# A graph-attention kernel on one core: the cross scores of two tiles packed into one 128x128 square and turned by one product instead of two

## The chip, the cores and the metric

The kernel runs on one core of a Trainium2 chip. A core has four computing engines that matter here: TensorE (PE in the profile; its weight loads have a row of their own, PEld), VectorE (DVE), ScalarE (ACT) and GpSimd (POOL). SyncE (SP) starts the transfers. Each engine works through its own list of instructions in order and waits on semaphores that others raise. The metric is the device time of the whole program in microseconds (us), lower is better; the median of three runs is given.

## What is computed

There are 128 graphs of 64 nodes, each node a row of 384 numbers, and one 64x64 adjacency matrix for each graph. A layer norm with a relu comes first, then two graph layers in a row, an addition to the input, another layer norm with a relu, a third graph layer, and a last addition. Each of the three graph layers does this:

```python
u = h @ h.T / sqrt(384)                      # 64 x 64 scores of a graph
a = softmax(u); delta = a * adjacency
attn = delta / (sum(delta) + 1e-10)
ctx = (attn above the diagonal) @ (h @ Wl.T + bl) \
    + diag(attn) * (h @ Ws.T + bs) \
    + (attn below the diagonal) @ (h @ Wr.T + br)
o = relu((ctx - mean) / sqrt(var + eps) * g + beta)
```

The three graph layers are the kernel's three phases. In all of them the scores are symmetric apart from rounding, which is split below.

## The kernel before

A tile is 128 rows, that is two graphs; a step handles two tiles (k = 0, 1), and a phase has 32 steps, so the program has 96. Each `body(s)` is one step, and on every engine the order of the calls in `body` is the order in which the engine works. Most steps of a phase run from a hardware loop of two bodies, the first two and the last four are written out. Work of several steps is interleaved: while step s is projected, step s+1 (`nxt`) is scored and masked, the output of step s-1 (`prev`) is normed, and the inputs of steps s+2 to s+4 are prepared.

Numbers are carried as a rounded part HI and a remainder LO, so every projection takes three products for each of three chunks of 384. One step on PE, in order: right projection of tile 0, `weigh` (attention times the projected rows) of the last step's tile 1, left and self projection of tile 0, the scores of `nxt` (six products of 256 columns), right projection of tile 1, `turn_cross(nxt)`, `weigh` of tile 0, left and self projection of tile 1. In phase 1 the left projection of tile 1 also has `spread_max` in it, a single product of 128 columns. `weigh` waits for `side_hi` and `side_lo` of the right side, does three products, waits for those of the left side and does three more. `side_lo` is what DVE's `split_side` raises (L828).

The scores of a tile pair need the term HI times HI plus HI times LO plus its mirror image. `scores` multiplies HI of a tile with HI and LO side by side, so `score_bank` holds for each tile a 128x128 square of HI.HI and a 128x128 square of HI.LO, the cross scores. The mirror image of the cross scores is made in four moves: ACT copies both squares to `cross` (`copy_cross`, L568, 128x256), PE turns them by a product with the identity and adds them onto the HI.HI squares in `score_bank` (`turn_cross`, L430, two products of 128 columns), and DVE adds the two (`sum_scores`, L764, one instruction for each half of the partitions) into `score`. Only the two 64x64 blocks on the diagonal of each square are scores of a graph; the others are left unused.

After that `score` goes on: in phases 0 and 2 (`bounded`) ACT takes the exponential straight away (`exponentials`, L585), and DVE masks it (`mask_edges`, L793). In phase 1 the row maximum comes first (`row_maximum` L771, `place_max` L776, `spread_max` on PE, `shift_scores` L785). POOL builds the edge blocks from the masked scores (L1010, L1014).

Other lines that are named below: on DVE L743 `turn_nodes` (waits for ACT's `fill_source`, L552 or L549), L726 `input_stats` (phases 0 and 2), L852 `centre`, L861 `norm`, L870 `residual` (phases 1 and 2), L730 the first instruction of `gather_input`, L747 `split_nodes`; on ACT L609 `split_side` and L603 `seed_side`; on PE L447 the projections and L478 `weigh`.

Of the kernel before, what the change touches and what calls it, by code (L numbers as in the profile page):

```python
# [32 lines left out]
F32 = mybir.dt.float32  # L33
# [5 lines left out]
P = 128  # L39
NODES = 64  # L40
# [87 lines left out]
def adj_gnn_program(nc, x, adj, weights, vectors, identity, triangles, out):  # L128
# [6 lines left out]
    with ctx:  # L135
# [55 lines left out]
        edge_bank = bank("edge_bank")  # L191
        first_bank = [edge_bank, score_bank]
        max_rows = edge_bank[:, 0:2 * NODES].rearrange("p (k i) -> p k i", k=2)
        score_copy = cross[:, :, 0:NODES]
        scores4 = score_bank[:, :].rearrange("p (k a j) -> p k a j", k=2, a=2)
        source = nodes[:, :].rearrange("p (k d) -> p k d", k=2)
# [36 lines left out]
        node_hi = sem("node_hi")  # L233
        node_lo = sem("node_lo")
        scored = sem("scored")
        cross_copied = sem("cross_copied")
        cross_turned = sem("cross_turned")
        score_summed = sem("score_summed")
        max_done = sem("max_done")
        max_placed = sem("max_placed")  # L240
# [164 lines left out]
        def _(pe):  # L405
            def transpose_first(s):
                at_least(pe, score_summed, 2 * s.n)
                for k in range(2):
                    pe.wait_ge(source_ready, s.tile(k) + 1)
                    for c in range(CH):  # L410
                        mm = nc.tensor.transpose(first_bank[k][:, c * P:(c + 1) * P], source[:, k, c * P:(c + 1) * P], ident)
                    mm.then_inc(first_moved, 1)
# [12 lines left out]

            def turn_cross(s):

                pe.wait_ge(cross_copied, s.n + 1)
                for k in range(2):
                    mm = nc.tensor.matmul(score_bank[:, k * 256:k * 256 + P], cross[:, k], ident_r[:, :],  # L430
                                          start=False, stop=True, skip_group_check=True)
                mm.then_inc(cross_turned, 1)

            def spread_max(s):

# [103 lines left out]
        def _(act):  # L539
# [24 lines left out]

            def copy_cross(s):
                act.wait_ge(scored, s.n + 1)
                at_least(act, score_summed, 2 * s.n)
                nc.scalar.activation(cross[:, :, :], scores4[:, :, 1, :], ACT.Copy).then_inc(cross_copied, 1)  # L568

            def totals(s):  # L570
                act.wait_ge(max_bias_done, s.n + 1 - PAIRS)
# [5 lines left out]
            def exponentials(s):  # L577
                if not s.bounded:
                    act.wait_ge(shift_done, s.n + 1 - PAIRS)
                    nc.scalar.activation(score[:, :, :], score[:, :, :], ACT.Exp, scale=SCALE).then_inc(exp_done, 2)  # L580
                    return
                act.wait_ge(score_summed, 2 * s.n + 2)
                at_least(act, den_done, s.tile(0) - 2)
                for k in range(2):
                    nc.scalar.activation(score[:, k], score[:, k], ACT.Exp, scale=SCALE,  # L585
                                         accum_out=total[:, s.parity, k:k + 1]).then_inc(exp_done, 1)
# [132 lines left out]
        def _(dve):  # L719
# [39 lines left out]

            def sum_scores(s):  # L760

                dve.wait_ge(cross_turned, s.n + 1)
                for h, half in enumerate(HALVES):
                    nc.vector.tensor_tensor(score[half], scores4[half, :, 0, h * NODES:(h + 1) * NODES],  # L764
                                            cross[half, :, h * NODES:(h + 1) * NODES].bitcast(F32),
                                            ALU.add).then_inc(score_summed, 1)

            def row_maximum(s):

                dve.wait_ge(score_summed, 2 * s.n + 2)  # L770
                nc.vector.tensor_reduce(row_max[:, :], score[:, :, :], op=ALU.max, axis=AX.X).then_inc(max_done, 1)  # L771

            def place_max(s):
# [104 lines left out]
            def first_step(s):  # L878
                nxt, second, third, fourth = s.ahead(1), s.ahead(2), s.ahead(3), s.ahead(4)
                split_side(s, 0, RIGHT)  # L880
                sum_scores(s)
                split_side(s, 0, LEFT)
                mask_edges(s)
                gather_stats(second)
                split_first(SELF)
                split_first_nodes(nxt)
                input_shift(second)
                diagonal(s)
                split_edges(s)
                gather_stats(third)  # L890
                turn_nodes(second)
                input_shift(third)
                split_side(s, 1, RIGHT)
                split_side(s, 1, LEFT)
                sum_scores(nxt)
                context_stats(s, 0)
                denominator(s, 0)
                turn_nodes(third)
                gather_moments(s, 0)
                mask_edges(nxt)  # L900
                centre(s, 0)
                gather_stats(fourth)
                input_shift(fourth)

            def body(s):
# [17 lines left out]
                split_edges(s)  # L923
                if prev.exists():
                    centre(prev, 1)
                if fourth.exists() and fourth.bounded:
                    input_stats(fourth, 0)
                    input_stats(fourth, 1)
                if prev.exists():
                    norm(prev, 0)  # L930
                if nxt.exists():
                    sum_scores(nxt)
                if nxt.exists() and not nxt.bounded:
                    row_maximum(nxt)
                    place_max(nxt)
# [153 lines left out]
```

## Time and profile before

| | |
|---|---|
| median of 3 runs | 1234.78 us (1233.87 to 1236.38) |
| the profiled execution, its own time | 1234.55 us |
| its span in the trace | 1232.8 us |
| PE busy | 1215.1 us, 99% |
| PE weight loads busy | 1208.2 us |
| DVE busy | 1089.1 us, 88% |
| ACT busy | 833.8 us, 68% |
| POOL busy | 323.5 us, 26% |
| granted PE clock, mean | 0.997 |

The time outside the span, 1.75 us, is the start and the end of the program. Busy shares are means over the whole span; the phases differ in what they ask of DVE, and the phases can be told apart by time: phase 0 runs to about 412 us, phase 1 to about 820 us, phase 2 to the end.

### The profile page before, as it was taken

What the parts mean: (1) busy time and instruction counts of PE and PEld (TensorE: products, weight loads), DVE (VectorE), ACT (ScalarE), POOL (GpSimd) and SP (SyncE); (2) the same over time, 40 slices, a digit from 0 to 9 for tenths busy, and PEclk for the clock granted to TensorE, in tenths of its full rate; (3) what the DMA queues carried; (4) which work ended last, traced back from release to release, by engine and by line L of the source; (5) the groups of instructions that cost most, each with busy time, mean ns of one, the idle gap of its engine ahead of it and who ended that gap; (6) DMA issues with size and microseconds to landing.
All of it is one profiled execution on the core that took longest, in us unless ns stands there. A gap on an engine that the chain in (4) does not pass through costs nothing.

```text
span 1232.8 us, 27495 instructions
## 1 busy us (share of the span) xinstructions
PE 1215.1 (99%) x7163; PEld 1208.2 (98%) x7163; DVE 1089.1 (88%) x3125; ACT 833.8 (68%) x2079; POOL 323.5 (26%) x438
## 2 busy tenths in 40 slices
PE   8999999999999999999999999999999999999997
PEld 7899999999999999999999999999999999999997
DVE  7888888888887889999999999999999999999986
ACT  6666666666767776666667676676666666666763
POOL 2322222222222221212112121342323232323221
PEclk9999999999999999999999999999999999999999
DMA  5433333333233333232323333432332323232331
GB/s 187 127 109 94 107 96 101 101 92 110 88 106 122 102 109 107 96 106 84 105 94 99 103 96 106 144 98 95 96 106 96 106 96 106 96 101 95 97 96 43
DMA packets 112899, 126.91 MB, mean 103 GB/s; under 512 B 11104, under 2 KB 100192, under 8 KB 112864
## 3 DMA queue, kind: packets, MB, share of 16 engines
q1 hardware_dynamic: 112864, 126.50, 32.9%
q8 instruction: 15, 0.25, 0.1%
q14 instruction: 20, 0.16, 0.0%
HBM read 76.91 MB, written 49.55 MB: 103 GB/s over the span
## 4 chain that ended last, share of the span: by engine, by line
PE 91%; DVE 3%; issue 3%; POOL 1%; DMA 1%; ACT 0%; SPq 0%; POOLq 0%; DVEq 0%; ACTq 0%
PE left_bank L447 23%; PE right_bank L447 23%; PE context_bank L447 23%; PE context_bank L478 16%; PE score_bank L422 5%; PE score_bank L430 1%; DMA rows<-weights 1%; DVE node_t L747 1%; DVE context L861 0%; POOL weight L1021 0%; DVE turned L743 0%; DVE in_stats L726 0%; DVE context L852 0%; DVE side_parts L828 0%; DVE score L764 0%
## 5 line engine op out<-in xcount | busy, mean ns | idle before, releaser
L447 PE MATMUL left_bank<-weight,node_t 128*128 128x384 f32 x1728 | 337.9, 338 | 0.0
L447 PE MATMUL context_bank<-weight,node_t 128*128 128x384 f32 x1728 | 332.7, 337 | 3.2 <-ACT context_bank L615 3.2
L447 PE MATMUL right_bank<-weight,node_t 128*128 128x384 f32 x1728 | 333.7, 338 | 1.0 <-ACT right_bank L603 0.6
L609 ACT ACTIVATE side_parts<-right_bank 128x384 fp32r<-128x384 f32 x192 | 94.4, 492 | 316.6 <-PE context_bank L478 316.6
L447 PEld LDWEIGHTS context_bank<-weight,node_t 128*128 128x128 f32 x1728 | 303.5, 189 | 3.7 <-ACT context_bank L615 3.5
L447 PEld LDWEIGHTS left_bank<-weight,node_t 128*128 128x128 f32 x1728 | 303.9, 188 | 0.0
L447 PEld LDWEIGHTS right_bank<-weight,node_t 128*128 128x128 f32 x1728 | 298.9, 188 | 2.1 <-issue 1.8
L478 PE MATMUL context_bank<-side_parts,attn_t 128*128 128x386 f32 x1152 | 240.7, 344 | 3.7 <-issue 3.4
L478 PEld LDWEIGHTS context_bank<-side_parts,attn_t 128*128 128x128 f32 x1152 | 199.0, 190 | 6.6 <-issue 5.7
L747 DVE TENSOR_TENSOR node_t<-nodes,node_t 128x768 fp32r<-128x768 f32 x94 | 119.8, 1275 | 18.1 <-ACT node_t L557 18.1
L1004 POOL TENSOR_TENSOR rstd<-spread,scalars 128x2 f32<-128x2 f32 x96 | 66.2, 689 | 257.6 <-DVE spread L844 257.6
L1014 POOL TENSOR_TENSOR edge_block<-edge,tri 128x512 f32<-128x512 f32 x96 | 133.3, 1388 | 0.0
L743 DVE STREAM_TRANSPOSE turned<-nodes 128x768 f32<-128x768 f32 x94 | 91.9, 978 | 44.4 <-ACT nodes L552 41.3
L621 ACT ACTIVATE context_bank<-context_bank,diag 128x386 f32<-128x386 f32 x192 | 105.1, 547 | 34.4 <-PE context_bank L447 33.6
L1010 POOL TENSOR_TENSOR own_edge<-edge,tri 128x128 f32<-128x128 f32 x96 | 46.8, 488 | 306.1 <-DVE edge L793 306.1
L852 DVE SCALAR_TENSOR_TENSOR context<-context_bank,moments,vector_rows 128x384 f32<-128x384 f32 x192 | 117.0, 609 | 2.4
L833 DVE BATCH_NORM_STATS2 stats<-context_bank 128x6 f32<-128x384 f32 x192 | 107.1, 558 | 12.0 <-PE context_bank L478 11.9
L828 DVE TENSOR_TENSOR side_parts<-right_bank,side_parts 128x384 fp32r<-128x384 f32 x192 | 106.6, 555 | 12.2 <-ACT side_parts L609 8.4
L828 DVE TENSOR_TENSOR side_parts<-left_bank,side_parts 128x384 fp32r<-128x384 f32 x192 | 102.7, 535 | 2.1 <-ACT side_parts L609 2.1
L998 POOL TENSOR_TENSOR in_spread<-in_moments,scalars 128x2 f32<-128x2 f32 x64 | 17.7, 277 | 304.4 <-DVE in_moments L731 304.4
L615 ACT ACTIVATE context_bank<-vector_rows 128x386 f32<-128x386 f32 x192 | 94.5, 492 | 0.0
L603 ACT ACTIVATE left_bank<-vector_rows 128x384 f32<-128x384 f32 x192 | 93.6, 488 | 0.0
(75 smaller groups left out, 1520.5 us busy)
## 6 DMA issues: line engine op xcount, KB each, us to landing
squares<-turned SPq DMA_DIRECT2D x94, 384.0 KB, 2.7
nodes<-squares SPq DMA_DIRECT2D x376, 96.0 KB, 2.2
rows<-x SPq DMA_DIRECT2D x64, 384.0 KB, 3.7
out<-rows SPq DMA_DIRECT2D x31, 384.0 KB, 2.6
adj_in<-adj SPq DMA_DIRECT2D x96, 64.0 KB, 1.9
piece<-weights SPq DMA_DIRECT2D x18, 192.0 KB, 2.6
rows<-weights SPq DMA_DIRECT2D x3, 576.0 KB, 7.8
vector_rows<-vectors SPq DMA_DIRECT2D x3, 384.0 KB, 7.0
```

The costliest lines, as they stand in the source:

```text
L447: mm = nc.tensor.matmul(bank[:, 0:D], node_t[:, s.parity, k, c, a], weight[:, s.phase % 2, w, c, b], start=False, stop=(c, a) == (CH - 1, ...
L478: mm = nc.tensor.matmul(context_bank[k][:, 0:DX], attn_t[:, a, k, 1 - side], side_parts[:, side, b], start=False, stop=(side == LEFT and a ...
L603: nc.scalar.activation(side_bank[side][k][:, 0:D], vector_row(s.phase, ROW_LEFT + side), ACT.Copy)\
L609: nc.scalar.activation(side_parts[:, side, HI, 0:D], side_bank[side][k][:, 0:D], ACT.Copy).then_inc(side_hi[side], 1)
L615: nc.scalar.activation(context_bank[k][:, 0:DX], vector_row(s.phase, ROW_SELF, 2), ACT.Copy)\
L621: nc.scalar.activation(context_bank[k][:, 0:DX], context_bank[k][:, 0:DX], ACT.Identity, scale=diag[:, s.parity, k:k + 1]).then_inc(self_s ...
L743: nc.vector.transpose(turned[:, :, :], source_blocks).then_inc(nodes_turned, 1)
L747: nc.vector.tensor_tensor(node_rows(s, LO), moved_rows, node_rows(s, HI).bitcast(F32), ALU.subtract).then_inc(node_lo, 1)
L828: nc.vector.tensor_tensor(side_parts[:, side, LO, 0:D], side_bank[side][k][:, 0:D], side_parts[:, side, HI, 0:D].bitcast(F32), ALU.subtrac ...
L833: nc.vector.bn_stats(stats[:, k], context_bank[k][:, 0:D]).then_inc(stats_done, 1)
L852: nc.vector.scalar_tensor_tensor(context[:, k], context_bank[k][:, 0:D], moments[:, k, 0:1], vector_row(s.phase, ROW_GAMMA), ALU.subtract, ...
L1014: nc.gpsimd.tensor_tensor(edge_block[:, :, :, :].rearrange("p k u (h j) -> p k (u h) j", h=2), edge[:, :, :].unsqueeze(2).to_broadcast([P, ...
```

## The change

`copy_cross` no longer copies both 128x128 cross squares. It copies only the diagonal blocks: two instructions (64 partitions, 2x64 elements) take, for each half of the partitions, the block that stands in its own half for both tiles, and two more (64 partitions, 64 elements) put those blocks of the first and last place where a packed square needs them. `cross[:, ...]` is looked at as four blocks of 64 columns, and the middle two are `cross_pack`, one 128x128 square with the four cross blocks of both tiles. `turn_cross` turns that square by one product, into the last 128 columns of `edge_bank`, with nothing added to it. `sum_scores` adds HI.HI and the copied cross block from `cross`, in two instructions as before, but it now waits for the four copies and no longer for PE. A new `add_cross` adds the turned block, one DVE instruction of 128x128 that reads `score` and `edge_bank`.

In DVE's `body`, `sum_scores(nxt)` moves ahead of `input_stats(fourth)` and `norm(prev, 0)`, and `add_cross(nxt)` stands where `sum_scores(nxt)` stood.

```diff
+        cross_blocks = cross[:, :, :].rearrange("p a (b j) -> p (a b) j", b=2)
+        cross_pack = cross_blocks[:, 1:3].rearrange("p b j -> p (b j)")
+        cross_here = [cross_blocks[half, 1 - h:4 - h:2] for h, half in enumerate(HALVES)]
+        turned_cross = edge_bank[:, 3 * P:4 * P].rearrange("p (k j) -> p k j", k=2)
...
             def turn_cross(s):
-                pe.wait_ge(cross_copied, s.n + 1)
-                for k in range(2):
-                    mm = nc.tensor.matmul(score_bank[:, k * 256:k * 256 + P], cross[:, k], ident_r[:, :],
-                                          start=False, stop=True, skip_group_check=True)
-                mm.then_inc(cross_turned, 1)
+                pe.wait_ge(cross_packed, 4 * (s.n + 1))
+                at_least(pe, cross_added, s.n)
+                nc.tensor.matmul(edge_bank[:, 3 * P:4 * P], cross_pack, ident_r[:, :],
+                                 start=True, stop=True, skip_group_check=True).then_inc(cross_turned, 1)
...
             def copy_cross(s):
                 act.wait_ge(scored, s.n + 1)
+                at_least(act, cross_turned, s.n)
                 at_least(act, score_summed, 2 * s.n)
-                nc.scalar.activation(cross[:, :, :], scores4[:, :, 1, :], ACT.Copy).then_inc(cross_copied, 1)
+                for h, half in enumerate(HALVES):
+                    nc.scalar.activation(cross_here[h], scores4[half, :, 1, half], ACT.Copy).then_inc(cross_packed, 1)
+                for h, half in enumerate(HALVES):
+                    nc.scalar.activation(cross_blocks[HALVES[1 - h], 1 + h], scores4[half, 1 - h, 1, half], ACT.Copy).then_inc(cross_packed, 1)
...
             def sum_scores(s):
-                dve.wait_ge(cross_turned, s.n + 1)
-                for h, half in enumerate(HALVES):
-                    nc.vector.tensor_tensor(score[half], scores4[half, :, 0, h * NODES:(h + 1) * NODES],
-                                            cross[half, :, h * NODES:(h + 1) * NODES].bitcast(F32),
-                                            ALU.add).then_inc(score_summed, 1)
+                dve.wait_ge(cross_packed, 4 * (s.n + 1))
+                for h, half in enumerate(HALVES):
+                    nc.vector.tensor_tensor(score[half], scores4[half, :, 0, half], cross_here[h].bitcast(F32),
+                                            ALU.add).then_inc(score_summed, 1)
+
+            def add_cross(s):
                 dve.wait_ge(cross_turned, s.n + 1)
+                dve.wait_ge(score_summed, 2 * s.n + 2)
+                nc.vector.tensor_tensor(score[:, :, :], score[:, :, :], turned_cross, ALU.add).then_inc(cross_added, 1)
```

The places that waited for `score_summed` before the exponentials and the row maximum now wait for `cross_added`; `transpose_first`, used at the program's start, waits for it too.

Instructions on DVE in the loop of phase 2, from L743 of one step on. Before:

```order
L743 STREAM_TRANSPOSE turned<-nodes 128x768
L828 TENSOR_TENSOR side_parts<-left_bank,side_parts 128x384
L821 TENSOR_TENSOR attn_t<-edge_block,attn_t 128x512
L852 SCALAR_TENSOR_TENSOR context<-context_bank,moments,vector_rows 128x384
L726 BN_STATS in_stats<-rows 128x6 x2
L861 SCALAR_TENSOR_TENSOR context<-context,rstd,vector_rows 128x384
L764 TENSOR_TENSOR score<-score_bank,cross 64x128 x2
L730 MEMSET scalars 128x1
```

And now, where the numbers of the lines have moved (L773 is `sum_scores`, L735 `input_stats`, L780 `add_cross`):

```order
L752 STREAM_TRANSPOSE turned<-nodes 128x768
L842 TENSOR_TENSOR side_parts<-left_bank,side_parts 128x384
L835 TENSOR_TENSOR attn_t<-edge_block,attn_t 128x512
L866 SCALAR_TENSOR_TENSOR context<-context_bank,moments,vector_rows 128x384
L773 TENSOR_TENSOR score<-score_bank,cross 64x128 x2
L735 BN_STATS in_stats<-rows 128x6 x2
L875 SCALAR_TENSOR_TENSOR context<-context,rstd,vector_rows 128x384
L780 TENSOR_TENSOR score<-score,edge_bank 128x128
L739 MEMSET scalars 128x1
```

The two sums stand three instructions earlier, and one instruction of 128x128 is new in their old place; nothing behind it has changed places.

Instructions on ACT in the loop of phase 0, from the scaling of tile 1's self rows to the next wait for PE. Before:

```order
L621 ACTIVATE context_bank<-context_bank,diag 128x386
L566 REGISTER_ALU
L98 REGISTER_ALU
L568 ACTIVATE cross<-score_bank 128x256
L603 ACTIVATE left_bank<-vector_rows 128x384
```

And now:

```order
L630 ACTIVATE context_bank<-context_bank,diag 128x386
L571 REGISTER_ALU
L98 REGISTER_ALU
L575 ACTIVATE cross<-score_bank 64x2x64 x2
L577 ACTIVATE cross<-score_bank 64x64 x2
L612 ACTIVATE left_bank<-vector_rows 128x384
```

One copy has become four shorter ones; the seed behind them, and the wait behind that, stand where they stood.

## Rows read from the trace of the kernel before

**Rows 1.** Windows, phases 0 to 2: length; busy PE, PEld, DVE, ACT, POOL; clock; DMA.

```profile
200.00:300.00 100.00, 100.00 (x596) 100.00 (x595) 83.98 (x258) 68.21 (x169) 26.44 (x40) 1.00 0.34 100
500.00:600.00 100.00, 100.00 (x598) 100.00 (x597) 94.55 (x249) 68.39 (x175) 18.81 (x24) 1.00 0.32 100
1000.00:1100.00 100.00, 100.00 (x594) 99.70 (x593) 91.44 (x274) 67.97 (x168) 30.14 (x41) 1.00 0.31 100
```

**Rows 2.** Timeline of phase 0, PE: start us, us, what; the start counts.

```profile
313.89 0.33 PE L430 MATMUL score_bank<-ident_r,cross 128*128 128x128 f32 x2
...
315.18 1.74 PE L447 MATMUL left_bank<-weight,node_t 128*128 128x384 f32 x9
319.88 1.21 PE L478 MATMUL context_bank<-side_parts,attn_t 128*128 128x386 f32 x6
320.93 1.74 PE L447 MATMUL left_bank<-weight,node_t 128*128 128x384 f32 x9
```

**Rows 3.** Timeline of phase 1, PE, around the single product of 128 columns.

```profile
617.70 0.22 PE L437 MATMUL edge_bank<-max_diag,same_graph 128*128 128x128 f32 x1
...
618.34 1.74 PE L447 MATMUL context_bank<-weight,node_t 128*128 128x384 f32 x9
```

**Rows 4.** Timeline of phase 2, ACT's copies and exponentials, PE's load for `turn_cross`.

```profile
1006.84 0.39 ACT L568 ACTIVATE cross<-score_bank 128x256 fp32r<-128x256 f32 x1
1007.12 0.49 ACT L603 ACTIVATE left_bank<-vector_rows 128x384 f32<-128x384 f32 x1
1007.97 0.37 PEld L430 LDWEIGHTS score_bank<-ident_r,cross 128*128 128x128 f32 x2
1010.50 0.25 ACT L585 ACTIVATE score<-score 128x64 f32<-128x64 f32 x1
```

**Rows 5.** Timeline of phase 1, DVE, `sum_scores` of two steps and neighbours.

```profile
602.29 0.60 DVE L861 SCALAR_TENSOR_TENSOR context<-context,rstd,vector_rows 128x384 f32<-128x384 f32 x1
603.14 0.61 DVE L764 TENSOR_TENSOR score<-score_bank,cross 64x128 f32<-64x128 f32 x2 [0.24 <-PE score_bank L430]
...
615.01 0.61 DVE L861 SCALAR_TENSOR_TENSOR context<-context,rstd,vector_rows 128x384 f32<-128x384 f32 x1
615.73 0.61 DVE L764 TENSOR_TENSOR score<-score_bank,cross 64x128 f32<-64x128 f32 x2
616.37 0.28 DVE L771 TENSOR_REDUCE row_max<-score 128x2 fp32r<-128x128 f32 x1
```

**Rows 6.** Timeline of phase 2, DVE and PEld, in order of time.

```profile
1005.21 0.98 DVE L743 STREAM_TRANSPOSE turned<-nodes 128x768 f32<-128x768 f32 x1 [0.77 <-ACT nodes L552]
...
1007.15 0.61 DVE L852 SCALAR_TENSOR_TENSOR context<-context_bank,moments,vector_rows 128x384 f32<-128x384 f32 x1
...
1009.78 0.06 DVE L730 MEMSET scalars<- 128x1 f32 x1
...
1013.92 0.55 DVE L828 TENSOR_TENSOR side_parts<-left_bank,side_parts 128x384 fp32r<-128x384 f32 x1
...
1014.31 0.74 PEld L478 LDWEIGHTS context_bank<-side_parts,attn_t 128*128 128x128 f32 x4
1014.58 0.47 PEld L478 LDWEIGHTS context_bank<-side_parts,attn_t 128*128 128x128 f32 x3
...
1017.71 0.98 DVE L743 STREAM_TRANSPOSE turned<-nodes 128x768 f32<-128x768 f32 x1 [0.75 <-ACT nodes L552]
```

**Rows 7.** Timeline of DVE near phase 1's end, `norm` and `sum_scores`.

```profile
792.67 0.60 DVE L861 SCALAR_TENSOR_TENSOR context<-context,rstd,vector_rows 128x384 f32<-128x384 f32 x1
793.19 0.60 DVE L764 TENSOR_TENSOR score<-score_bank,cross 64x128 f32<-64x128 f32 x2
...
807.19 0.60 DVE L764 TENSOR_TENSOR score<-score_bank,cross 64x128 f32<-64x128 f32 x2
```

**Rows 8.** Timeline of DVE, phase 1, `shift_scores`, of the new instruction's shape.

```profile
619.33 0.29 DVE L785 TENSOR_TENSOR score<-score,edge_bank 128x128 f32<-128x128 f32 x1
619.64 0.56 DVE L870 SCALAR_TENSOR_TENSOR rows<-context,rows 128x384 f32 x1
```

More of the change, by code:

```diff
@@ L235, in adj_gnn_program @@
         scored = sem("scored")
-        cross_copied = sem("cross_copied")
+        cross_packed = sem("cross_packed")
         cross_turned = sem("cross_turned")
+        cross_added = sem("cross_added")
         score_summed = sem("score_summed")
@@ L426, in turn_cross @@
             def turn_cross(s):
-                pe.wait_ge(cross_copied, s.n + 1)
-                for k in range(2):
-                    mm = nc.tensor.matmul(score_bank[:, k * 256:k * 256 + P], cross[:, k], ident_r[:, :],
-                                          start=False, stop=True, skip_group_check=True)
-                mm.then_inc(cross_turned, 1)
+                pe.wait_ge(cross_packed, 4 * (s.n + 1))
+                at_least(pe, cross_added, s.n)
+                nc.tensor.matmul(edge_bank[:, 3 * P:4 * P], cross_pack, ident_r[:, :],
+                                 start=True, stop=True, skip_group_check=True).then_inc(cross_turned, 1)
             def spread_max(s):
@@ L581, in exponentials @@
                     return
-                act.wait_ge(score_summed, 2 * s.n + 2)
+                act.wait_ge(cross_added, s.n + 1)
                 at_least(act, den_done, s.tile(0) - 2)
@@ L760, in sum_scores @@
             def sum_scores(s):
+                dve.wait_ge(cross_packed, 4 * (s.n + 1))
[3 more added lines that the diff above has]
+            def add_cross(s):
                 dve.wait_ge(cross_turned, s.n + 1)
-                for h, half in enumerate(HALVES):
-                    nc.vector.tensor_tensor(score[half], scores4[half, :, 0, h * NODES:(h + 1) * NODES],
-                                            cross[half, :, h * NODES:(h + 1) * NODES].bitcast(F32),
-                                            ALU.add).then_inc(score_summed, 1)
+                dve.wait_ge(score_summed, 2 * s.n + 2)
+                nc.vector.tensor_tensor(score[:, :, :], score[:, :, :], turned_cross, ALU.add).then_inc(cross_added, 1)
             def row_maximum(s):
-                dve.wait_ge(score_summed, 2 * s.n + 2)
+                dve.wait_ge(cross_added, s.n + 1)
                 nc.vector.tensor_reduce(row_max[:, :], score[:, :, :], op=ALU.max, axis=AX.X).then_inc(max_done, 1)
@@ L881, in first_step @@
                 sum_scores(s)
+                add_cross(s)
                 split_side(s, 0, LEFT)
@@ L895, in first_step @@
                 sum_scores(nxt)
+                add_cross(nxt)
                 context_stats(s, 0)
@@ L925, in body @@
                     centre(prev, 1)
+                if nxt.exists():
+                    sum_scores(nxt)
                 if fourth.exists() and fourth.bounded:
@@ L931, in body @@
                 if nxt.exists():
-                    sum_scores(nxt)
+                    add_cross(nxt)
                 if nxt.exists() and not nxt.bounded:
```

## The prediction

> **What bounds the kernel now.** I read the windows first, one from the middle of each phase [rows 1]. PE is busy for the whole 100 us in all three, at the full granted clock; the weight loads are too, except in phase 2, where 0.3 us are missing. DVE is at 84, 95 and 91 of 100. So PE sets the pace, but DVE is a close second in phases 1 and 2, and what the change takes from PE it gives to DVE. The question for each phase is whether DVE, or a chain through DVE, has a shorter period than PE will have.
>
> I read that from the timeline. In phase 1 the only place where DVE waits for PE is `sum_scores`: `norm` starts at 615.01 and `sum_scores` 0.72 us later, in the other step at 602.29 and 0.85 us later [rows 5]. Where DVE does not wait, the two stand 0.52 us apart (792.67 to 793.19, [rows 7]; rows of 0.6 us overlap by some 0.08). So DVE idles 0.20 and 0.33 us, 0.27 on average, in a step of 12.59 (603.14 to 615.73, [rows 5]). Everything else that DVE waits for in that phase is POOL or ACT work that DVE itself released. **DVE's own period in phase 1 is about 12.59 - 0.27 = 12.32 us.**
>
> In phase 2 DVE has a visible wait at L743 of 0.77 and 0.75 us, for ACT's `nodes` [rows 6]. It looks like slack and is not. From L743 at 1005.21 DVE runs without a stop to `split_side` of the left side, which ends at 1013.92 + 0.55 = 1014.47. PE, in the middle of `weigh`, starts its third load at 1014.31 and the fourth, the one that needs this result, at 1014.58: 0.27 us later where 0.175 is normal. So PE already waits about 0.1 us for DVE here. When `weigh` is done ACT can read the next right projection and seed, and the `nodes` that it writes after that release L743 at 1017.71. That is a **closed chain**, L743 on DVE, left split, `weigh` on PE, ACT, L743, and its period is 1017.71 - 1005.21 = 12.50 us. In the next step PE does not wait, by a hair, so PE and the chain tie. Phase 0 has no `residual` on DVE and no such tie: DVE has 16 us in 100, some 2 us a step, free [rows 1].
>
> **The change part by part.**
>
> *PE loses one product of 128 columns a step.* The two now cost 315.18 - 313.89 = 1.29 us with the `weigh` behind them, and a `weigh` without them takes 320.93 - 319.88 = 1.05 [rows 2], so 0.24 for two. What one alone costs in this stream is shown by `spread_max`: from 617.70 to 618.34 are 0.64 us for it and three projections at 1.05 / 6 = 0.175, which leaves 0.115 [rows 3, 2]. Saved: 0.24 - 0.12 = **0.12 us a step**.
>
> The Trainium skill's page "TensorE: Matmul & The Clock Gate", section "Back-to-back issue gap", gives about 81 ns for each load and product of 128 columns in a sustained stream; by that the saving would be 0.08 us a step and the total some 1.2 us later than mine. The row of this kernel is dearer, and I go by the row.
>
> *ACT makes four copies instead of one.* A copy of 128x256 takes 0.39 us and the next starts after 0.28, so rows overlap by 0.11; one of 64 elements takes 0.25 [rows 4]. Between them, 128 elements take about 0.30. Two starts at 0.20 apart, one at 0.15, and a last row of 0.25 put the end at 0.20 + 0.20 + 0.15 + 0.25 = 0.80 us behind the start. PE's load for `turn_cross` stands 1007.97 - 1006.84 = 1.13 us behind it [rows 4], so PE does not wait, with 0.33 to spare. ACT's extra 0.45 us lie ahead of its long wait for PE and cost nothing.
>
> *DVE gets `add_cross` and moves the sums.* Its shape stands in phase 1 already: `shift_scores`, 128x128 out of `score` and `edge_bank`, takes 0.29 us and holds the next one up for 0.31 [rows 8]. Bounds: 0.19 us if it overlaps as other rows do (0.1 less), 0.32 if the next one depends on it, as `row_maximum` does. The sums read what they read before and keep 0.61 us for two. In phase 2 they now come up at 1007.15 + 0.52 = 1007.67, when the four copies end at 1006.84 + 0.80 = 1007.64 and their semaphore has still to arrive: 0 to 0.1 us of waiting. Before, L852 to L730 takes 1009.78 - 1007.15 = 2.63 us [rows 6] for `centre`, two `input_stats`, `norm` and two sums; the same ones stand there after, in another order, and the add's 0.31 come on top. So **DVE pays 0.31 us a step**, with 0.2 to 0.4 for the bounds and the wait together. It no longer waits for PE at this place.
>
> **The sum, by stages**, against the profiled 1234.55 us.
> - Phase 0, 31 steps: DVE's 0.31 lie in its 2 us, PE saves 0.12: **-3.7**.
> - Phase 1, 28 steps up to where input statistics start again: PE would need 12.59 - 0.12 = 12.47, DVE 12.32 + 0.31 = 12.63. DVE is late by 0.16 a step until the gap to PE is used up, two steps, and from then on sets the pace: 26 x (12.63 - 12.59) = +1.0, -0.2 for the first two: **+0.8**.
> - Four steps around the start of phase 2, which are DVE-bound now (807.19 - 793.19 = 14.00 us for a step, the sums 0.52 behind `norm`, so no wait for PE, [rows 7]): 4 x 0.31 = **+1.2**.
> - Phase 2, 26 steps: the chain goes through `add_cross` but not through `turn_cross`, which PE does elsewhere in the step, while ACT and DVE work. It pays the 0.31 and gets nothing back, less some 0.02 because in every other step it does not bind yet: 12.50 + 0.29 = 12.79, and 26 x 0.29 = **+7.5**.
> - The last four steps have no inputs to prepare, DVE has room: **-0.5**.
>
> Together +5.3: 1234.55 + 5.3 = 1239.9, **1240 us**. The profiled run is 0.2 us below the median, so that holds for the median too. 0.2% of this kernel, 2.5 us, is about what a measurement can tell from no change.
>
> **The rivals.**
> - *DVE's cost is small* (the add overlaps, 0.15 to 0.2 us in all). Phase 1 then stays with PE: 12.32 + 0.18 = 12.50 against 12.59, -2.5; phase 2 gets 0.18 - 0.02 = 0.16 longer, x 26 = +4.2; with -3.7, +0.7 and -0.5 that is -1.8, 1233 us. For it: in most rows of DVE the next starts early. Against it: the same shape, `shift_scores`, does not [rows 8].
> - *DVE's waits are real slack, PE is the only bound* (the other side: faster). Then all steps but the four save 0.12: 92 x 0.12 = 11, 1223.5 us. For it: PE is at 100 of 100 and DVE waits 0.75 us a step in phase 2. Against it: the late fourth load [rows 6]. It decides from the point where the chain of phase 2 has 0.3 us of room.
> - *The copies are late.* If each holds ACT up as long as the 128x256 one does, 0.28, the last ends at 3 x 0.28 + 0.30 = 1.14 us, a hundredth behind PE's load, and with the semaphore PE waits 0.1 a step and gives back what it saved; the sums in phase 2 wait another 0.35. That gives 0 + 0.8 + 1.2 + 26 x 0.64 = +18.6, 1253 us. Against it: ACT's rows shorten with their length [rows 4].
> - *The new waits tie POOL's work to DVE's in a worse way.* `mask_edges` and POOL's edge blocks come 0.3 us later in phase 0; were 0.3 a step exposed there, 31 x 0.3 = +9, 1249 us. The free 2 us speak against it.
>
> **How the numbers follow.** My forecast (chain of phase 2 pays, 1236 to 1244) 0.60; small DVE cost, 1230 to 1236, 0.17; PE alone, 1224, 0.07; late copies, 0.08; POOL, 0.04; something not seen, either way, 0.04. Leaving out PE alone and half of the dearest gives 1230 to 1249. Faster by over 0.2% (below 1232.3): 0.07 + a third of 0.17 + 0.02 = 0.14. Within 0.2%: the rest of the small cost and the lowest of my own, 0.17. Slower: 0.69.
>
> **What the profile after would show.** In phase 0 a step of 12.35 us with PE still at 100 of 100. In phase 1 no wait of DVE at the sums or the add, and PE waiting in `weigh` for the left split, step 12.6 to 12.65. In phase 2 PE's gap before the fourth load of `weigh` growing from 0.1 to about 0.4 us, a step near 12.8, while L743 keeps its wait of 0.75. The four copies ending 0.8 us behind the first one's start, ahead of PE's load. I am wrong if phase 2's step stays under 12.6, which happens if the add takes less than 0.15 us of DVE's time or if PE reaches the fourth load with room that I misread, or if PE waits for `cross_packed`.

## The result

The changed kernel takes 1243.98 us (median of 6 runs, 1243.53 to 1245.62); the kernel before, timed beside it, 1235.51 us (6 runs, 1233.87 to 1236.83). The ratio is 1.0073, 95% interval 1.0061 to 1.0085: **slower by 8.5 us**. I had said 1240.0, between 1230 and 1249, and most likely slower (0.69).

The profiled execution took 1245.62 us, span 1243.8 us, the highest of the six, 1.6 us above the median; that of before was 1.0 us below its median. So the two traces differ by 11.0 us where the medians differ by 8.5. The stages behind the 4th product make up 8.1 of the 11.0; of the start's 2.9 the medians leave about 0.4, known only to some 1.5 either way. Stages are compared by the starts of numbered products of `turn_cross` (1st, 4th, 32nd, 61st, 65th, 91st, 96th), and most of the excess stands before the 4th.

| us between starts | before | after | difference | predicted |
|---|---|---|---|---|
| program start to the 4th | 52.09 | 55.02 | +2.9 | -0.4 |
| phase 0, 28 steps | 349.08 | 345.72 | -3.36 | -3.4 |
| phase 1, 29 steps | 365.31 | 366.32 | +1.0 | +0.8 |
| four steps around the start of phase 2 | 53.83 | 55.74 | +1.9 | +1.2 |
| phase 2, 26 steps | 325.22 | 333.10 | +7.9 | +7.5 |
| last five | 62.40 | 63.18 | +0.8 | -0.5 |

The windows of the three phases after the change, same columns as [rows 1]:

```profile
200.00:300.00 100.00, 100.00 (x594) 100.00 (x593) 86.72 (x266) 74.57 (x196) 26.71 (x41) 1.00 0.33 100
500.00:600.00 100.00, 100.00 (x586) 98.23 (x585) 95.87 (x255) 72.10 (x199) 18.55 (x23) 1.00 0.32 100
1000.00:1100.00 100.00, 98.19 (x571) 95.88 (x570) 91.29 (x276) 70.81 (x188) 29.25 (x39) 1.00 0.31 99
```

Phase 0 is still PE's alone, with both rows at 100. In phase 1 the weight loads have gaps, and DVE is at 96. In phase 2 PE itself has gaps now: the row that stood at 100 is at 98.19, and the loads went from 99.70 to 95.88. DVE's share did not rise there, though it has more to do: it waits longer too.

The timeline of phase 0, PE, `scores` of two steps in a row (start, length, what):

```profile
299.66 0.87 PE L428 MATMUL score_bank<-node_t 128*128 128x256 f32 x6
...
312.00 0.87 PE L428 MATMUL score_bank<-node_t 128*128 128x256 f32 x6
```

12.34 us a step; 28 steps of before took 349.08, or 12.467 each, and 28 of after 345.72, or 12.347. The product that went is worth 0.120 us.

The timeline of phase 2 after the change, DVE, ACT and PEld, one step (answers to [rows 4] and [rows 6]):

```profile
1011.94 0.98 DVE L752 STREAM_TRANSPOSE turned<-nodes 128x768 f32<-128x768 f32 x1 [0.77 <-ACT nodes L557]
...
1013.57 0.57 ACT L575 ACTIVATE cross<-score_bank 64x128 fp32r<-64x128 f32 x2
1013.88 0.61 DVE L866 SCALAR_TENSOR_TENSOR context<-context_bank,moments,vector_rows 128x384 f32<-128x384 f32 x1
1014.16 0.46 ACT L577 ACTIVATE cross<-score_bank 64x64 fp32r<-64x64 f32 x2
...
1014.66 0.61 DVE L773 TENSOR_TENSOR score<-score_bank,cross 64x128 f32<-64x128 f32 x2 [0.17 <-ACT cross L577]
1014.70 0.19 PEld L436 LDWEIGHTS edge_bank<-ident_r,cross 128*128 128x128 f32 x1
...
1016.23 0.60 DVE L875 SCALAR_TENSOR_TENSOR context<-context,rstd,vector_rows 128x384 f32<-128x384 f32 x1
...
1016.87 0.29 DVE L780 TENSOR_TENSOR score<-score,edge_bank 128x128 f32<-128x128 f32 x1
...
1017.72 0.55 DVE L842 TENSOR_TENSOR side_parts<-right_bank,side_parts 128x384 fp32r<-128x384 f32 x1
...
1020.57 0.54 PEld L483 LDWEIGHTS context_bank<-side_parts,attn_t 128*128 128x128 f32 x3
1021.01 0.55 DVE L842 TENSOR_TENSOR side_parts<-left_bank,side_parts 128x384 fp32r<-128x384 f32 x1
...
1021.67 0.47 PEld L483 LDWEIGHTS context_bank<-side_parts,attn_t 128*128 128x128 f32 x3 [0.55 <-issue]
...
1024.80 0.98 DVE L752 STREAM_TRANSPOSE turned<-nodes 128x768 f32<-128x768 f32 x1 [0.74 <-ACT nodes L557]
```

Three things are to be seen. L752 keeps its wait of 0.77 and 0.74 us while the step grows to 12.86 us here: the wait is part of the circle and no slack. The chain's end is where it was forecast: the left split ends at 1021.56 and the fourth load of `weigh` starts at 1021.67, and PEld stood idle for 0.55 us before it. And what was not forecast: the four copies end at about 1014.62, 1.05 us behind the first one's start, and the sums, which would have started 0.52 us behind `centre` at 1014.40, start at 1014.66. **DVE loses 0.26 us to ACT in each step**, inside the chain (the row shows 0.17 of it as idle; the rest is the overlap with `centre` that is lost). PE's load for `turn_cross` at 1014.70 just does not wait.

### The profile page after: what moved, and what is told of

Same layout as the page of the kernel before. It is cut to its first block, busy times and chain, and to the rows that moved or that the text cites. A ratio compares the mean times of both kernels' runs of the same rounds, so it can differ in the third digit from the quotient of the medians.

```text
span 1243.8 us, 28008 instructions
## 1 busy us (share of the span) xinstructions
PE 1216.8 (98%) x7067; PEld 1195.4 (96%) x7067; DVE 1111.1 (89%) x3221; ACT 893.6 (72%) x2367; POOL 323.6 (26%) x438
## 4 chain that ended last, share of the span: by engine, by line
PE 45%; issue 24%; DVE 19%; ACT 5%; POOL 3%; DVEq 2%; DMA 0%; ACTq 0%; POOLq 0%; SPq 0%
PE right_bank L452 11%; PE context_bank L452 11%; PE left_bank L452 11%; PE context_bank L483 8%; DVE context L875 4%; PE score_bank L428 3%; DVE side_parts L842 3%; DVE stats L847 2%; DVE context L866 2%; POOL edge_block L1032 1%; DVE node_t L756 1%; POOL own_edge L1028 1%; ACT nodes L557 1%; DVE in_stats L735 1%; DVE score L773 1%
## 5 line engine op out<-in xcount | busy, mean ns | idle before, releaser
L483 PE MATMUL context_bank<-side_parts,attn_t 128*128 128x386 f32 x1152 | 248.6, 347 | 10.1 <-DVE side_parts L842 6.8
L483 PEld LDWEIGHTS context_bank<-side_parts,attn_t 128*128 128x128 f32 x1152 | 195.9, 189 | 24.1 <-issue 20.9
L752 DVE STREAM_TRANSPOSE turned<-nodes 128x768 f32<-128x768 f32 x94 | 91.9, 978 | 43.7 <-ACT nodes L557 40.7
L630 ACT ACTIVATE context_bank<-context_bank,diag 128x386 f32<-128x386 f32 x192 | 104.8, 546 | 25.9 <-PE context_bank L452 25.3
L612 ACT ACTIVATE right_bank<-vector_rows 128x384 f32<-128x384 f32 x192 | 91.8, 478 | 0.8 <-DMA vector_rows<-vectors 0.8
```

The source lines that it names most:

```text
L483: mm = nc.tensor.matmul(context_bank[k][:, 0:DX], attn_t[:, a, k, 1 - side], side_parts[:, side, b], start=False, stop=(side == LEFT and a ...
L612: nc.scalar.activation(side_bank[side][k][:, 0:D], vector_row(s.phase, ROW_LEFT + side), ACT.Copy)\
L630: nc.scalar.activation(context_bank[k][:, 0:DX], context_bank[k][:, 0:DX], ACT.Identity, scale=diag[:, s.parity, k:k + 1]).then_inc(self_s ...
L752: nc.vector.transpose(turned[:, :, :], source_blocks).then_inc(nodes_turned, 1)
```

## The experiments

All were timed beside the kernel before on the same chip. Its median was 1235.66 us (25 runs) beside the first four, 1235.13 (29) beside the next four and 1235.02 (15) beside the last two. Each kernel ran 8 to 10 times, one_product 4 and mixed 5. Line numbers shift by a few between kernels. The stages of all of them, in us as in the table above:

| kernel | to the 4th | phase 0 | phase 1 | four | phase 2 | last five |
|---|---|---|---|---|---|---|
| before | 52.09 | 349.08 | 365.31 | 53.83 | 325.22 | 62.40 |
| after | 55.02 | 345.72 | 366.32 | 55.74 | 333.10 | 63.18 |
| one_product | 53.80 | 345.72 | 361.66 | 53.72 | 324.38 | 62.05 |
| dve_only | 52.12 | 349.08 | 365.47 | 54.63 | 327.71 | 62.68 |
| two_copies | 54.68 | 345.72 | 366.04 | 55.14 | 326.76 | 62.33 |
| old_place | 53.47 | 345.72 | 363.17 | 55.22 | 327.78 | 62.46 |
| act_more | 54.37 | 349.08 | 365.36 | 53.86 | 325.24 | 62.40 |
| packed0 | 54.36 | 345.72 | 365.21 | 53.85 | 325.25 | 62.41 |
| packed01 | 54.46 | 345.72 | 363.32 | 55.21 | 325.28 | 62.42 |
| add_first | 54.43 | 345.72 | 362.19 | 54.40 | 329.18 | 62.65 |
| mixed | 54.20 | 345.72 | 362.22 | 54.39 | 325.21 | 62.40 |
| two_waits | 52.61 | 349.08 | 365.31 | 53.94 | 325.18 | 62.37 |

**one_product**: PE's part of the change alone, on the kernel before (tile 1 goes without the mirror image of its cross scores).

```diff
-                for k in range(2):
+                for k in range(1):
                     mm = nc.tensor.matmul(score_bank[:, k * 256:k * 256 + P], cross[:, k], ident_r[:, :],
```

> The kernel before with one of the two turning products left out (the cross scores of tile 1 are not turned, so its scores are not the reference's); DVE and ACT do what they did. My theory: 0.12 us a step saved where PE is the bound, in phase 0 (-3.7) and phase 1 (-3.4, since DVE's 12.33 us there are below PE's 12.47), nearly nothing in phase 2 where the chain already ties (12.46 against 12.50, -1), -0.5 in the last four steps: -8 to -9 us, 1227 us. The rival, PE alone is the bound: 92 x 0.12, -11 us, 1224 us. If the product costs only what its 0.08 us from start to start say: -5 us, 1230 us.

Measured 1227.32 us, ratio 0.9927 (0.9911 to 0.9944). Phase 0 gives the full 0.120 us a step, phase 1 0.126 (365.31 - 361.66 over 29), phase 2 only 0.03 (325.22 - 324.38 over 26). PE alone would take 12.347 us a step if its work there is that of phase 0, and phase 2 takes 12.476: there the chain sets the step, and with PE relieved nothing more is to be had. With two products PE alone would take 12.467 and the step is 12.508, 0.03 us above the chain's own. "DVE's waits are real slack" falls here.

**dve_only**: the kernel before, with an addition of the new one's shape behind the sums (it adds columns of the unturned cross scores once more).

```diff
+                dve.wait_ge(score_summed, 2 * s.n + 2)
+                nc.vector.tensor_tensor(score[:, :, :], score[:, :, :], scores4[:, :, 1, 0:NODES], ALU.add).then_inc(cross_added, 1)
```

> The kernel before with one DVE instruction more, of the shape of add_cross and at its place, and nothing taken from PE or added to ACT (it adds the first 64 columns of each unturned cross square once more to the scores, so the scores are not the reference's). My theory, that DVE's own period binds in phase 1 and the chain through the left split in phase 2: PE gives nothing, phase 0 stays at 12.47 us a step, phase 1 gets about 0.1 us a step longer, phase 2 about 0.3, the four steps between them 0.3 each, in all +9 to +11 us, 1245 us. The rival, that DVE's waits are slack and PE alone is the bound: within 1 us of before.

Measured 1238.56 us, ratio 1.0026 (1.0016 to 1.0035): +2.9 us where I expected three times that. The timeline of its phase 2, DVE:

```profile
1009.41 0.61 DVE L855 SCALAR_TENSOR_TENSOR context<-context_bank,moments,vector_rows 128x384 f32<-128x384 f32 x1
...
1011.38 0.60 DVE L765 TENSOR_TENSOR score<-score_bank,cross 64x128 f32<-64x128 f32 x2
1012.01 0.29 DVE L769 TENSOR_TENSOR score<-score,score_bank 128x128 f32<-128x128 f32 x1
1012.23 0.18 DVE L732 BATCH_NORM_AGGREGATE in_moments<-in_stats 128x2 f32<-128x6 f32 x1
...
1013.02 0.55 DVE L831 TENSOR_TENSOR side_parts<-right_bank,side_parts 128x384 fp32r<-128x384 f32 x1
```

The add takes 0.29 us, but what follows starts 0.22 behind it, and of that some is won back before the right split. From `centre` to the right split are 3.61 us here and 3.47 in one_product (1013.66 to 1017.13): the add costs the chain **0.14 us** and not 0.31. The rows of one_product:

```profile
1013.66 0.60 DVE L852 SCALAR_TENSOR_TENSOR context<-context_bank,moments,vector_rows 128x384 f32<-128x384 f32 x1
...
1017.13 0.56 DVE L828 TENSOR_TENSOR side_parts<-right_bank,side_parts 128x384 fp32r<-128x384 f32 x1
```

Phase 1, where I expected 0.1 us a step, grew by 0.16 us in all 29.

**two_copies**: the kernel after, in which ACT makes both copies of the lower half first and each sum waits only for the two copies of its half.

```diff
-                dve.wait_ge(cross_packed, 4 * (s.n + 1))
                 for h, half in enumerate(HALVES):
+                    dve.wait_ge(cross_packed, 4 * s.n + 2 * h + 2)
...
                     nc.scalar.activation(cross_here[h], scores4[half, :, 1, half], ACT.Copy).then_inc(cross_packed, 1)
-                for h, half in enumerate(HALVES):
```

> The changed kernel with the four copies reordered, both that read the lower half of the partitions first, and the first sum waiting for two copies and the second for four, so DVE does not wait at the sums. If the copies' lateness (0.26 us between where the sums could start and where they do in phase 2) is part of what makes phase 2 slow: 0.2 us a step back there, 26 steps, -5 us against the changed kernel, 1239 us, phases 0 and 1 as they were. If only the add's own time counts: no change from 1244 us.

Measured 1236.7 us, ratio 1.0012 (1.0002 to 1.0021), 7.3 us below after's median, more than the 5 that I expected. The copies still end late, and DVE no longer waits for them, in the timeline of phase 2:

```profile
1008.83 0.27 ACT L575 ACTIVATE cross<-score_bank 64x128 fp32r<-64x128 f32 x1
1009.12 0.21 ACT L576 ACTIVATE cross<-score_bank 64x64 fp32r<-64x64 f32 x1
1009.36 0.27 ACT L575 ACTIVATE cross<-score_bank 64x128 fp32r<-64x128 f32 x1
1009.66 0.22 ACT L576 ACTIVATE cross<-score_bank 64x64 fp32r<-64x64 f32 x1
```

```profile
1009.14 0.61 DVE L865 SCALAR_TENSOR_TENSOR context<-context_bank,moments,vector_rows 128x384 f32<-128x384 f32 x1
1009.66 0.60 DVE L772 TENSOR_TENSOR score<-score_bank,cross 64x128 f32<-64x128 f32 x2
...
1012.72 0.55 DVE L841 TENSOR_TENSOR side_parts<-right_bank,side_parts 128x384 fp32r<-128x384 f32 x1
```

Phase 2 loses 6.3 of its 7.9 us, the four steps 0.6 of 1.9 and the last five 0.85, all they had. **The wait for the copies was most of the change's cost.**

**old_place**: the kernel after, with the two sums back behind `norm`, right ahead of the add.

```diff
-                if nxt.exists():
-                    sum_scores(nxt)
                 if fourth.exists() and fourth.bounded:
                     input_stats(fourth, 0)
...
                 if nxt.exists():
+                    sum_scores(nxt)
                     add_cross(nxt)
```

> The changed kernel with the two sums put back in their old place, right ahead of the add. DVE then doesn't wait for the copies, and the add no longer starts 0.12 us late behind the norm. My theory: phase 2 loses the 0.26 us wait and gains a little at the add, about 12.66 us a step in place of 12.85, -5 us; phase 1 hardly moves; 1239 us. The rival, that moving the sums early is what keeps the cost of the add down (its operands are ready): slower than 1244 us by 0.1 us a step, 1250 us.

Measured 1235.27 us, ratio 0.9996 (0.9986 to 1.0005): better than expected, and 8.7 us below after. There is no wait for copies in this place, and `centre` to the right split is 3.62 us (1005.80 to 1009.42), as in dve_only. Phase 1 gains too, 366.32 to 363.17: there the order was the cost, since no wait for copies shows in after. With the add in this place DVE's step in phase 1 is at most 363.17 / 29 = 12.52 us.

**act_more**: the kernel before, with two copies of 64 partitions ahead of the full copy.

```diff
+                for h, half in enumerate(HALVES):
+                    nc.scalar.activation(cross[half, :, half], scores4[half, :, 1, half], ACT.Copy).then_inc(first_copies, 1)
+                act.wait_ge(first_copies, 2 * s.n + 2)
                 nc.scalar.activation(cross[:, :, :], scores4[:, :, 1, :], ACT.Copy).then_inc(cross_copied, 1)
```

> The kernel before with two copies of 64 partitions and 2x64 elements ahead of the full copy on ACT, some 0.65 us more of ACT a step, the full copy ending about 1.05 us behind the first one's start, ahead of PE's load at 1.13; DVE and PE as before. My theory, that ACT's time there is hidden by its wait for PE: within 1 us of 1235.7. The rival, that the later start of the seed behind it or of the turn reaches PE: 0.1 us a step or more, 1245 us.

Measured 1235.2 us, ratio 0.9999 (0.9989 to 1.0008): more work on ACT, and a seed that starts later, cost nothing from the 4th product on. In phase 2 the full copy ends 0.99 us behind the first one's start (1009.21 to 1010.20), and PE's load stands at 1010.34, so the turn itself was not late. What is left for the copies of after is DVE's wait.

**packed0** and **packed01**: the kernel old_place in phase 0, or in phases 0 and 1; the code of before in the rest.

```diff
+                if s.phase >= 1:
+                    pe.wait_ge(cross_copied, s.n + 1 - 1 * PAIRS)
+                    for k in range(2):
+                        mm = nc.tensor.matmul(score_bank[:, k * 256:k * 256 + P], cross[:, k], ident_r[:, :],
+                                              start=False, stop=True, skip_group_check=True)
+                    mm.then_inc(cross_turned, 1)
+                    return
```

with the like in `copy_cross` and `sum_scores`, and no `add_cross` there.

> Packed copies, one product and the add in phase 0 only, the sums in their old place; phases 1 and 2 as in the kernel before. My theory: phase 0 gives 3.4 us from the 4th to the 32nd step, 1 to 2 us of it go in the program's first 50 us, nothing changes after: 1233.5 us. The rival, that the start takes nothing on average: 1232 us.

> Packed in phases 0 and 1, old form in phase 2, the sums in their old place. My theory: phase 0 -3.4, phase 1 -2.1 (363.2 in place of 365.3 us for 29 steps, DVE's own period there being 12.52), the start +1 to +2, phase 2 as before: 1231.5 us, faster than both kernels. The rival, that DVE's load in phase 1 spoils the steps around phase 2's start by as much: 1234 us.

Measured: packed0 1232.09 us, ratio 0.9976 (0.9965 to 0.9987), at the rival's 1232; packed01 1233.1, 0.9984 (0.9975 to 0.9994), nearer to its rival's 1234 than to my 1231.5. Packing pays where PE alone sets the pace. In phase 1 packed01 gains 2.0 us and gives 1.4 back in the four steps behind, which DVE sets; in all, nothing that shows in the medians.

**add_first**: two_copies with the add ahead of `norm` instead of behind it.

```diff
+                if nxt.exists():
+                    add_cross(nxt)
                 if prev.exists():
                     norm(prev, 0)
-                if nxt.exists():
-                    add_cross(nxt)
```

> The changed kernel with the copies in the order of two_copies and the add ahead of the norm instead of behind it, in all phases. In the runs so far the add never starts before the norm ahead of it has ended (0.65 us behind its start, where 0.52 is usual). If that 0.12 us is the price of this neighbour: phase 1 at 12.50 us a step in place of 12.62 (-3.4 us against two_copies), phase 2 by 0.0 to 0.1 us a step shorter, 1232 to 1233 us. If the price goes with the add wherever it stands: 1236.7 us, as two_copies.

Measured 1234.33 us, ratio 0.9990 (0.9980 to 1.0000), a little above what I expected. Against two_copies phase 1 fell by 3.85 us, to 0.5 us above one_product's; phase 2 rose by 2.4. The timeline of phase 2, DVE, shows why:

```profile
1005.57 0.61 DVE L865 SCALAR_TENSOR_TENSOR context<-context_bank,moments,vector_rows 128x384 f32<-128x384 f32 x1
1006.09 0.60 DVE L772 TENSOR_TENSOR score<-score_bank,cross 64x128 f32<-64x128 f32 x2
1006.72 1.02 DVE L734 BATCH_NORM_STATS2 in_stats<-rows 128x6 f32 x2
1007.77 0.29 DVE L779 TENSOR_TENSOR score<-score,edge_bank 128x128 f32<-128x128 f32 x1
1007.98 0.61 DVE L874 SCALAR_TENSOR_TENSOR context<-context,rstd,vector_rows 128x384 f32<-128x384 f32 x1
...
1009.25 0.55 DVE L841 TENSOR_TENSOR side_parts<-right_bank,side_parts 128x384 fp32r<-128x384 f32 x1
```

The add starts 1.05 us behind `input_stats`, where `norm` starts 0.93 behind in dve_only (1009.93 to 1010.86): it overlaps with nothing ahead of it. `centre` to the right split is 3.68 us.

**mixed**: add_first's order in phases 0 and 1, the code of before in phase 2.

> Packed in phases 0 and 1 with the sums early and each pair of sums waiting for its own copies, the add ahead of norm; phase 2 with the code of before. If an instruction on DVE costs what its neighbours make of it, phase 1 gets 12.49 us a step as in add_first (362.2 us for 29 steps against 365.3 before), phase 0 saves 0.12 a step, phase 2 stays at 325.2, the four steps between cost about 0.6 more: -3.4 -3.1 +0.6 and +1 at the start is 1230 to 1231 us, 1.5 to 2 below packed0 (1232.1). The rival is that each saving in phase 1 is given back at the hand-over to phase 2, as in packed01: then it is no faster than packed01 (1233.1).

Measured **1230.79 us, ratio 0.9963 (0.995 to 0.9977)**, as expected, and the fastest of all that compute the whole reference, though its interval and packed0's overlap. Phase 1 takes 362.2 us, the four steps 54.4.

**two_waits**: the kernel before, where the first sum also waits for a semaphore value of the step before.

```diff
                 dve.wait_ge(cross_turned, s.n + 1)
+                at_least(dve, score_summed, 2 * s.n)
                 for h, half in enumerate(HALVES):
```

> The kernel before, in which the first of the two sums also waits for score_summed of the step before, a value reached long ago. Two theories of why the add never overlaps the instruction ahead of it (0.63 us from norm's start to its own, where the sums stood 0.52 behind norm). (a) A second wait, or a wait on DVE's own semaphore, holds an instruction until the one ahead is done: then norm to the sums becomes 0.63 to 0.66, the chain of phase 2 is 0.11 longer (centre to right split 3.58 instead of 3.47) and, by period = 12.46 + lengthening, its step goes from 12.51 to 12.57, +1.6 us; about 1237. (b) The hold comes from what the add reads or writes: then the sums stay 0.52 behind norm and the time stays 1235.

Measured 1235.6 us, ratio 1.0003 (0.9994 to 1.0013); in the timeline of its phase 2 the sums still start 0.51 us behind `norm`:

```profile
1009.23 0.60 DVE L862 SCALAR_TENSOR_TENSOR context<-context,rstd,vector_rows 128x384 f32<-128x384 f32 x1
1009.74 0.60 DVE L765 TENSOR_TENSOR score<-score_bank,cross 64x128 f32<-64x128 f32 x2
```

A second wait that is already met costs nothing; theory (a) falls. That something in the add's operands holds it, theory (b), is not shown by this.

**The chain's law.** For each kernel, one step's stretch from `centre` to the right split, its excess over one_product's 3.47, and the mean step of phase 2:

| kernel | stretch | 12.476 + excess | step measured |
|---|---|---|---|
| one_product | 3.47 | 12.476 | 12.476 |
| two_copies | 3.58 | 12.59 | 12.568 |
| dve_only | 3.61 | 12.62 | 12.604 |
| old_place | 3.62 | 12.63 | 12.607 |
| add_first | 3.68 | 12.69 | 12.661 |
| after | 3.84 | 12.85 | 12.812 |

Within 0.04 us all follow the stretch, each a little short of it, by about a tenth of the excess (0.09 of 0.11, 0.34 of 0.37; why is open), whether PE has one product (five of them) or two (dve_only). That is what a closed chain would do.

## Why the prediction was right, and where it was off

**PE saves 0.12 us a step: right.** 0.120, to three digits, in phase 0 of every kernel with one product. By the page "TensorE: Matmul & The Clock Gate" of the Trainium skill, section "Back-to-back issue gap", an estimate would have been 0.08. The trace disagrees with it in this stream.

**Phase 1, DVE's own period 12.63 us: the number right, its parts not.** Measured 366.32 / 29 = 12.63. I had it from 12.32 + 0.31; with the add in its old place the step is 12.52, so there the add is worth 0.20, as far as the 12.32 holds, which no run measured. The rest is the new order. The timeline of after, phase 1:

```profile
602.05 0.61 DVE L866 SCALAR_TENSOR_TENSOR context<-context_bank,moments,vector_rows 128x384 f32<-128x384 f32 x1
602.57 0.60 DVE L773 TENSOR_TENSOR score<-score_bank,cross 64x128 f32<-64x128 f32 x2
603.20 0.62 DVE L875 SCALAR_TENSOR_TENSOR context<-context,rstd,vector_rows 128x384 f32<-128x384 f32 x1
603.86 0.29 DVE L780 TENSOR_TENSOR score<-score,edge_bank 128x128 f32<-128x128 f32 x1
604.18 0.29 DVE L785 TENSOR_REDUCE row_max<-score 128x2 fp32r<-128x128 f32 x1
```

`norm` stands 0.63 us behind the sums, the add 0.66 behind `norm` where the sums stood 0.52 [rows 7], and `row_maximum` 0.32 behind the add. From `centre` to `row_maximum` are 2.13 us, and 2.01 in old_place (611.42 to 613.43). I had said that PE would wait in `weigh` for the left split. It does so in one step, by 0.11 us (the loads at 621.59 and 621.88); in the other it waits 0.17 us ahead of the first load, at 608.74, right behind ACT's L630 (608.02 + 0.54), which came late because ACT had waited 0.85 us for DVE's `shift_scores`.

**Phase 2, a closed chain that gets nothing back from PE: the mechanism right, its parts mis-sized.** The step that failed is the end of the four copies, "0.20 + 0.20 + 0.15 + 0.25 = 0.80 us behind the start", and, from it, "0 to 0.1 us of waiting". The copies end 1.05 us behind (1013.57 to 1014.62), because no copy starts before the one ahead of it has ended, which I had let them do: they start 0.29, 0.24 and 0.30 us apart in two_copies, for rows of 0.27, 0.21 and 0.27. The wait is 0.26 us. The other term, "DVE pays 0.31 us a step", is 0.14 in phase 2 (dve_only) and 0.11 in two_copies' order. 0.26 + 0.11 = 0.37 us more chain. The step before was 0.03 us longer than the chain's own, and in the table above the step grows 0.03 less than the stretch, which leaves the 0.30 measured. I had 0.29 from 0.31. **Two errors cancelled**: phase 2's +7.5 against +7.9 looks better than it was, and that is luck. PEld's idle time ahead of the fourth load is 0.55 us where I had 0.4, which fits PE being ready 0.12 us sooner: I had left that out of this figure. Without the wait phase 2 costs 1.5 us (two_copies).

**The four steps, +1.2: +1.9 measured**; of the excess 0.6 is the same wait. **The last five, -0.5: +0.8 measured.** I said DVE had room. one_product gains only 0.35 there, and two_copies, without the wait, stands at -0.07: the wait is 0.85 and takes what was to be won.

**The program's start, which I left out but for -0.4: +2.9** in the profiled run, and about 0.4 by the medians. The profiles differ there by up to 2.9 us between kernels, as told below.

**The rivals.** PE alone (1223.5) fell by the idle PEld in phase 2 and by one_product. The small cost of DVE (0.15 to 0.2) was in truth half right: as to the add in phase 2 it held, 0.14. The late copies (1.14 us) were nearly right as to their size, 1.05, and wrong as to PE, which does not wait: they reach the time through DVE. POOL's wait in phase 0 did not come; the step there is 12.35. A rival that joined the two, a small add and late copies, is what happened in phase 2, and I had not put them together.

## What to carry to other kernels

A wait in front of an instruction is no slack when what it waits for was released by the same engine's own work: add up the circle, and price an edit by how much longer the circle gets. Taking work off the busiest engine pays only in stages that no other engine or chain holds: here mixed, which packs in phases 0 and 1, is at 0.9963, and add_first, the same packed code in all three phases, at 0.9990. When one instruction is split over several shorter ones that others wait for, order the pieces and let each consumer wait for its own: that was worth 7.3 of the 8.5 us here.

## What was not expected of the hardware

**No copy on ACT starts before the row ahead of it ends.** A copy of 64x64 is 0.21 to 0.22 us long and the next starts after 0.24; one of 64x128 is 0.27 long, the next starts after 0.29 to 0.30. I had taken an overlap of 0.11 from the 128x256 copy [rows 4], but that is the overlap of the seed behind it. The 128x256 copy itself began only when the row ahead of it had ended, in before:

```profile
1006.28 0.55 ACT L621 ACTIVATE context_bank<-context_bank,diag 128x386 f32<-128x386 f32 x1
1006.84 0.39 ACT L568 ACTIVATE cross<-score_bank 128x256 fp32r<-128x256 f32 x1
1007.12 0.49 ACT L603 ACTIVATE left_bank<-vector_rows 128x384 f32<-128x384 f32 x1
```

And the seed starts early behind the last 64x64 copy too, in after:

```profile
1014.16 0.46 ACT L577 ACTIVATE cross<-score_bank 64x64 fp32r<-64x64 f32 x2
1014.53 0.48 ACT L612 ACTIVATE left_bank<-vector_rows 128x384 f32<-128x384 f32 x1
```

So the half partitions are not shown to be the reason; what holds a copy back is open. The page "ScalarE: Activation LUTs" of the Trainium skill, section "What ACT_TABLE_LOAD costs", says that ACTIVATEs in a row overlap by about 93 ns. The trace agrees for the seed behind a copy (0.11 and 0.09 us), and not for the copies.

**The new add never overlaps what stands ahead of it.** Most rows of 0.60 us let the next start after 0.52. The add starts 0.63 to 0.66 behind `norm` or the sums and 1.05 behind `input_stats`, in all places tried. A met second wait is not the reason (two_waits). In before, the second of the two sums does not overlap the first either (they start 0.31 us apart, the first is 0.27 to 0.28 long), and it has no wait of its own. Whether the add's wait for the sums plays a part was not tried; the cause stays open.

**The first 50 us vary from kernel to kernel.** Windows of 35 to 40 us, before and then after (same columns as [rows 1]):

```profile
35.00:40.00 5.00, 5.00 (x26) 5.00 (x25) 4.55 (x11) 3.36 (x8) 0.69 (x1) 0.73 0.56 181
```

```profile
35.00:40.00 5.00, 3.50 (x12) 3.50 (x13) 4.18 (x11) 4.24 (x9) 0.69 (x1) 0.50 0.56 176
```

In both, PE was busy for under 2 of the 5 us ahead of this window (1.80 and 1.65). In the one the granted clock in it is 0.73 and 26 matmuls are recorded, in the other 0.50, which is the lower level of 1.2 GHz, and 12. It is 0.50 or 0.51 too in one_product, two_copies, packed0 and add_first, 0.66 in old_place and act_more, 0.70 in packed01 and mixed, 0.73 in two_waits and 0.79 in dve_only. Kernels with one product a step reach the 4th product 1.4 to 2.9 us later than before, and act_more, with two, 2.3 us later. The clock of this window alone does not order them: packed01 and mixed stand at 0.70 and are 2.4 and 2.1 us late, one_product at 0.51 and is 1.7 late. No run was made to move the clock, so whether it explains the difference is open. Much of it is the single execution's: the medians, less the stages behind the 4th product, leave 0.4 us at the start for after, nothing for act_more, 1.8 for packed01 and 1.7 for mixed, each known only to between 1 and 2 us.
